# Output projection: which engine adds the skip row and the positive branch of a tile

## What is computed

```
x = x + _L0_gnn_ref(_layernorm(x, axis=-1), adj, ...)
x = x + _L0_ffn_ref(_layernorm(x, axis=-1)[None], ...)[0]
...
    hidden = jnp.einsum('hij,jhd->ihd', attn, seq).reshape(N, D_IN)
    hidden = hidden @ W_out + b_out
    return jax.nn.elu(hidden)
```

## Time and profile before

| | |
|---|---|
| median of 3 runs | 1024.69 us (1024.34 to 1026.82) |
| the profiled execution | 1023.84 us, span 1022.0 us |
| TensorE (PE) busy | 991.0 us, 97% |
| VectorE (DVE) busy | 791.2 us, 77% |
| ScalarE (ACT) busy | 664.3 us, 65% |
| GpSimd (POOL) busy | 359.7 us, 35% |
| output projection | from about 469 to 540 us of the span |

### The profile page before, as it was taken

How to read it: one execution, slowest core, us unless ns; L and a number is a source line. 1 busy time by engine, 2 the same in 40 slices (tenths; PEclk the granted TensorE clock), 3 DMA queues, 4 the chain that set the end, 5 groups by cost and what they waited for, 6 DMA issues and landing times.

```text
span 1022.0 us, 27171 instructions
## 1 busy us (share of the span) xinstructions
PE 991.0 (97%) x11243; PEld 880.8 (86%) x11243; DVE 791.2 (77%) x1175; ACT 664.3 (65%) x995; POOL 359.7 (35%) x312
## 2 busy tenths in 40 slices
PE   6998999999999999999999999999999999999998
PEld 5877999999999999997777888888888877878887
DVE  6799999999999999965996334457766579966554
ACT  4489999999999999715775334344455556645431
POOL 3111467677667666754530000000264000016400
PEclk9999999999999999999999999999999999999999
DMA  9940111111111111803772000110163224452332
GB/s 246 107 79 33 65 44 45 63 44 44 44 56 52 44 44 44 269 27 112 247 235 116 1 1 1 35 49 1 57 210 105 60 92 129 132 185 86 91 130 100
DMA packets 53600, 89.99 MB, mean 88 GB/s; under 512 B 5904, under 2 KB 30096, under 8 KB 52976
## 3 DMA queue, kind: packets, MB, share of 16 engines
q1 hardware_dynamic: 43104, 67.26, 19.5%
q0 software_dynamic: 7296, 12.59, 6.9%
q10 hardware_dynamic: 3088, 8.49, 2.6%
HBM read 74.82 MB, written 26.08 MB: 99 GB/s over the span
## 4 chain that ended last, share of the span: by engine, by line
PE 45%; DVE 5%; DMA 2%; issue 1%; ACT 1%; SPq 0%; POOL 0%; DVEq 0%; ACTq 0%
PE bank L1849 17%; PE bank L1370 17%; PE bank L1926 2%; PE bank L1877 1%; PE bank L1878 1%; PE bank L1880 1%; DVE hid L1164 1%; DMA xs<-sorted_latent_rows 1%; PE bank L695 1%; PE bank L1896 1%; PE bank L1834 1%; DVE hid L1161 1%; PE bank L1832 1%; DMA xr<-in_x 1%; DVE stat L1166 1%
## 5 line engine op out<-in xcount | busy, mean ns | idle before, releaser
L757 ACT ACTIVATE arena<-arena 128x1024 fp8e4<-128x1024 f32 x320 | 336.9, 1135 | 2.4 <-ACT arena L749 1.4
L1010 PE MATMUL bank<-arena 128*128 128x132 f16 x4096 | 284.4, 221 | 8.0 <-DVE arena L857 6.6
L1010 PEld LDWEIGHTS bank<-arena 128*128 128x128 fp8e4 x4096 | 245.0, 97 | 9.8 <-DVE arena L857 7.8
L1370 PE MATMUL bank<-xt,up_parts 128*128 128x512 f32 x768 | 187.8, 394 | 1.9 <-DVE up_parts L1354 1.9
L953 POOL TENSOR_TENSOR arena<-arena 128x264 f32<-128x264 f32 x64 | 150.9, 2377 | 104.2 <-DVE arena L828 83.6
L1849 PE MATMUL bank<-down_parts,h_parts 128*128 128x512 f32 x768 | 184.5, 389 | 0.1
L1014 PE MATMUL bank<-arena 128*128 128x66 f16 x4096 | 172.9, 195 | 0.0
L1370 PEld LDWEIGHTS bank<-xt,up_parts 128*128 128x128 f32 x768 | 143.4, 189 | 31.0 <-issue 2.1
L1849 PEld LDWEIGHTS bank<-down_parts,h_parts 128*128 128x128 f32 x768 | 144.0, 188 | 30.3 <-issue 0.5
L828 DVE TENSOR_SCALAR arena<-arena 128x1024 uint8<-128x1024 f32 x192 | 156.7, 882 | 0.0
L1014 PEld LDWEIGHTS bank<-arena 128*128 128x128 fp8e4 x4096 | 154.1, 98 | 0.0
(11 more groups left out here) (244 smaller groups left out, 1363.7 us busy)
## 6 DMA issues: line engine op xcount, KB each, us to landing
arena<-s_rows SPq DMA_DIRECT2D x32, 512.0 KB, 3.5
sorted_latent_rows<-zeros SPq DMA_DIRECT2D x1, 4992.0 KB, 18.4
xs<-sorted_latent_rows SPq DMA_DIRECT2D x39, 128.0 KB, 2.1
sorted_expert_rows<-expert_y SPq DMA_DIRECT2D x39, 128.0 KB, 1.7
arena<-in_adjT POOLq DMA_DIRECT2D x8, 512.0 KB, 26.9
xr<-in_x SPq DMA_DIRECT2D x16, 256.0 KB, 3.7
x_rows<-hid SPq DMA_DIRECT2D x16, 256.0 KB, 3.2
up_sb<-in_upT ACTq DMA_DIRECT2D x4, 1024.0 KB, 5.3
```

The source lines that it names most:

```text
L757: last = nc.scalar.activation(m8[:, k, j, :], s1b[:, k % 2, :], ACT.Sigmoid, bias=bias_now[:, k % 2, j:j + 1], scale=STEEP, saturate=False)
L1010: last = nc.tensor.matmul(o, m8[:, k, j, i * P:(i + 1) * P], vs[:, b, j, :], start=(j == 0), stop=(j == T - 1))
L1370: last = nc.tensor.matmul(bank[6 + s % 2][:, :], sa[:, s % 2, a, k, :], xt[c][:, b, k, :], start=(i == 0), stop=(i == len(mm) - 1))
```

## The change

The addition of xr and pos moves from VectorE to GpSimd (`skip`). VectorE then finishes x1 with one instruction: neg - 1 + x1. A semaphore skip_ready tells VectorE that GpSimd is done, and the waits on xr, pos and hn move with the addition. GpSimd's stream for step t becomes `normalise(t + 1)`, `root(t - 3)`, `skip(t - 2)`. The semaphore neg_step is replaced by act_step, which had been used once before; ScalarE's instructions and their order stay the same.

```
-                nc.scalar.activation(neg[:, t % 2, :], bank[2 + t % 2][:, :], ACT.Relu, scale=-1.0).then_inc(neg_step, 1)
+                nc.scalar.activation(neg[:, t % 2, :], bank[2 + t % 2][:, :], ACT.Relu, scale=-1.0).then_inc(act_step, 1)
                 nc.scalar.activation(pos[:, t % 2, :], bank[2 + t % 2][:, :], ACT.Relu).then_inc(pos_ready, 1)
-                act.wait_ge(neg_step, t + 1)
+                act.wait_ge(act_step, t + 2)
...
+            def skip(t):
+
+                pool.wait_ge(xr_loaded[t % 2], 16 * (t // 2 + 1))
+                pool.wait_ge(pos_ready, t + 1)
+                pool.wait_ge(hn_ready, t + 1)
+                nc.gpsimd.tensor_tensor(x1[:, t, :], xr[:, t % 2, :], pos[:, t % 2, :], ALU.add).then_inc(skip_ready, 1)
+
             for t in range(T + 3):
                 if t == 3:
                     normalise(pool, 3)
                 if 3 <= t < T - 1:
                     normalise(pool, t + 1)
                 if t >= 3:
                     root(t - 3)
+                if 2 <= t < T + 2:
+                    skip(t - 2)
...
             def residual(t):
 
-                dve.wait_ge(xr_loaded[t % 2], 16 * (t // 2 + 1))
-                dve.wait_ge(pos_ready, t + 1)
-                dve.wait_ge(hn_ready, t + 1)
-                step(nc.vector.scalar_tensor_tensor(out=x1[:, t, :], in0=xr[:, t % 2, :], scalar=-1.0,
-                                                    in1=pos[:, t % 2, :], op0=ALU.add, op1=ALU.add))
+                dve.wait_ge(skip_ready, t + 1)
                 dve.wait_ge(e_ready, t + 1)
-                nc.vector.tensor_tensor(x1[:, t, :], x1[:, t, :], neg[:, t % 2, :], ALU.add).then_inc(x1_ready, 1)
+                nc.vector.scalar_tensor_tensor(out=x1[:, t, :], in0=neg[:, t % 2, :], scalar=-1.0, in1=x1[:, t, :],
+                                               op0=ALU.add, op1=ALU.add).then_inc(x1_ready, 1)
```

More of the change, by code:

```diff
@@ L647, in build @@
             "wo_high", "wo_low", "ht_low", "x1_stored", "x1_stored_late"))
-        rden_ready, hn_ready, ht_in_psum, ht_copied, y_in_psum, pos_ready, neg_step, e_ready = (sem(n) for n in (
-            "rden_ready", "hn_ready", "ht_in_psum", "ht_copied", "y_in_psum", "pos_ready", "neg_step", "e_ready"))
+        rden_ready, hn_ready, ht_in_psum, ht_copied, y_in_psum, pos_ready, e_ready = (sem(n) for n in (
+            "rden_ready", "hn_ready", "ht_in_psum", "ht_copied", "y_in_psum", "pos_ready", "e_ready"))
         x1_ready, var2_ready, std2_ready, xn2_ready, xt2_in_psum, xth_copied, xtl_ready = (sem(n) for n in (
@@ L703, in build @@
         act_passed = sem("act_passed")
+        skip_ready = sem("skip_ready")
         bias_copied, scaled_step = sem("bias_copied"), sem("scaled_step")
```

## The result

The changed kernel takes 1037.82 us (median of 6 runs, 1035.84 to 1040.25), the kernel before 1025.74 us in 6 runs of its own. The ratio is 1.0119, with a 95% interval from 1.0101 to 1.0137. The change makes the kernel slower by 12.1 us. The forecast was 8.1 us slower, 1032.8 us; the measured median lies 0.3 us above the upper end of the range (1037.5). The direction and the mechanism were right. The size was too small, because the skip takes 1.29 us and not the 1.05 us of the forecast.

The account below looks back on a forecast made before the run. VectorE bounds the output projection at 4.38 us a tile; a GpSimd-VectorE loop of 4.86 us, 4.00 in the last tiles, delays the last root by 8.1 us: 1024.69 + 8.1 = 1032.8 us, range 1024.5 to 1037.5.

Parts of the forecast that it names:

- What bounds the kernel: Output projection: VectorE sets the pace at 4.38 us a tile; TensorE alone could do 3.87.
- The closed loop: GpSimd and VectorE: add, statistics, variance, root, skip, add form a loop of 4.86 us a tile, 4.00 in the last four.
- The collision: VectorE's add waits for GpSimd's normalisation right behind the skip, ending 0.56 us after it, at K + 2.62 from skip start K.
- The cost of the skip: GpSimd's added 128x512 addition takes 1.05 us, like the normalisation; bounds 0.68 and 1.59 us.
- if L1151 isn't about 1.05: Sign named as proving the prediction wrong: GpSimd's skip row not lasting about 1.05 us.
- The sum: Turns added over the tiles: last root at 545.3 instead of 537.19 us, so everything behind comes 8.1 us later.
- I see no reason for another distance: From GpSimd's last root to TensorE's third product it stays 3.30 us.
- nothing gives it back: From the third product on TensorE is busy almost without a break, so the 8.1 us delay remains.
- The range: Execution time between 1024.5 and 1037.5 us, from the first rival's result up to part of the costlier cases.
- The costlier one: Rival, 10 in 100: skip dearer than the normalisation (up to 1040.9 us), or idle TensorE granted less clock (1038 or 1039).
- VectorE did not get in ahead of the normalisation: Rival, 12 in 100: VectorE's add starts before GpSimd's normalisation, takes 0.68 us, loop 4.00 us throughout; 1024.6 us.
- The loop did not stay open: Rival, 6 in 100: roots and skips keep ahead of VectorE, TensorE sets 3.87 us a tile; 4.9 us saved, 1019.8.

Follow-up runs that it names:

- Experiment 2: Changed kernel with GpSimd's skip of the next tile ahead of the root instead of behind it: 1023.43 us, ratio 0.9963 to the kernel before.
- experiment 6: Kernel of Experiment 2 with the load of xr issued once the skip has read its buffer, ahead of the store of x1: 1019.15 us, ratio 0.9936.
- experiment 3: Changed kernel with both the normalisation's wait of experiment 1 and the skip-before-root order of Experiment 2: 1023.7 us, ratio 0.9962.
- experiment 1: Changed kernel with each normalisation from tile 5 on waiting until VectorE has finished the tile before it: 1031.99 us, ratio 1.0048.
- Experiment 4: Changed kernel with the skip in four forms by tile: multiplication, broadcast second operand, 16 pieces, half width; one execution, 1034.58 us, read for lengths alone.
- Experiment 5: Changed kernel, same order, with the skip's second operand as 16 broadcast columns of pos in all 16 tiles: 1034.52 us, ratio 1.0087.
- the second pair: The kernel before and the changed kernel, both unaltered, profiled once more; start of stage to third product took 71.42 and 83.94 us.

## Why the prediction was wrong in its size and right in its mechanism

**What bounds the kernel.** Right. VectorE set the pace in the kernel before, and experiments 2 and 6 show that TensorE's 3.87 us is the next bound.

**The closed loop.** Right. Experiment 2 removes the loss by moving the skip ahead of the root, but with it the collision; experiment 3 against experiment 1, neither of which has the collision, shows that the order alone is worth 8 to 9 us, 1.4 of them by the clock of the third product. Its parts came as forecast: from the end of the add (499.75 + 1.52 = 501.27) to the next skip (503.52) it is 2.25 us, against the forecast's 0.03 + 0.73 + 0.22 + 0.23 + 1.03 = 2.24.

**The collision.** Right, shown by experiment 1. The forecast had the add end 1.57 us behind the skip (2.62 - 1.05); it ends 1.56 us behind it.

**The cost of the skip.** This is the step that failed, a term of the sum that was mis-sized: "The nearest has the same size, two SBUF inputs and one SBUF output: the normalisation, 1.05 us alone ... I take 1.05." The normalisation reads its second operand as 16 columns broadcast over 32. Experiment 4 gave the skip such an operand, and it took 1.05 us; with two dense operands it takes 1.29. (The normalisation itself was not run with a dense one.) The shape in the row of the trace (128x512 from 128x512) doesn't show this; the code did. The 0.24 us stand in the chain 16 times, 3.8 us. It is also one of the signs that the prediction named for being wrong: "if L1151 isn't about 1.05".

**The sum.** At the last root, counted from the start of the stage, the forecast was 8.1 us late and the profile is 12.6. Of the 4.5 us between, 3.8 are the skip's length. The remaining 0.7 are small starts: the first skip began 0.24 us behind pos instead of 0.03, one skip was issued 0.22 us late, and about 0.2 us is spread over the turns. Experiment 5 bears this out from the other side. Giving the skip its 1.05 us takes 3.8 us out of the stage. With this one term put right the sum would have given 8.1 + 3.8 = 11.9 us, close to the 12.1 measured, but partly by luck, since the small starts and the third product of the next paragraph pull in opposite directions.

**"I see no reason for another distance."** The distance from the last root to the third product was right (3.31 us). That product's own length was not thought of. It is 1.6 us shorter (1.4 in the second pair), since the granted clock stayed up. That contradicts "nothing gives it back". So at its end the third product is 12.6 - 1.6 = 11.0 us later than before. This lies within the 10.4 to 14.1 us that the ratio's interval gives; the median of 12.1 lies 1.1 us above it.

**The range.** The prediction's upper bound for the skip, 1.59 us, gave 1040.9, and the range stopped short of that, at 1037.5. The forecast also stood on a median of 1024.69 from three runs, where six gave 1025.74; that is 1.0 us of the miss. With an unknown that counts 16 times, 0.1 us of its length is 1.6 us of the time, and the forecast's own range of 1030.5 to 1035 allowed for an error of 0.1 us a loop.

**The rivals.** The costlier one, at 10 in 100, came true in its first half: the skip was dearer than the normalisation. Its second half did not: the clock never fell inside the stage, and at the third product it stayed up where it had fallen before. VectorE did not get in ahead of the normalisation in any of the 11 tiles. The loop did not stay open. The load of xr was never waited for in the changed kernel, as assumed.

## What to carry to other kernels

When an addition moves to an engine with time to spare, look at what stands ahead of it in that engine's stream before looking at its price. Here the same instructions on GpSimd gave 1.2% slower behind the root, 0.5% slower there with one more wait, and 0.4% faster ahead of it. If what stands ahead waits for the consumer's last result, the two streams close into a loop, and every instruction's length in it counts in each turn, even though both engines show idle time. And take the price of an instruction from a row with the same operands, dense or broadcast, and not only the same shape.

## What the hardware showed unexpectedly

- On GpSimd, an addition of 128x512 with both inputs dense took 1.27 to 1.33 us. With the second input broadcast from 16 columns it took 1.04 to 1.05 us. Multiplication and addition took the same.
- TensorE's granted clock behind a gap does not follow from the gap's length alone. Ahead of the third product it was idle for 1.87 us in both profiles of the kernel before, and the product took 4.58 and 4.37 us, with the granted clock at 0.50 for part of it. It was idle for 2.02 us there in the changed kernel (two profiles) and in experiments 4 and 5, and the product took 2.98 to 3.01 us. In experiment 1 it was idle for 2.02 us as well, and the product took 4.38. In experiment 2 TensorE had been busy without a gap for over 32 us when it fell idle for 2.45 us, and the granted clock went to 0.50 behind that. Where the clock stayed up, TensorE had waited longer for VectorE in the tiles before: 10.4 to 13.8 us from 464 to 558 us, against 7.9 in experiment 1 and 3.4 in the kernel before. No run here separates that from other differences, and the cause stays open.
